# A graph network on one core: the attention stages' rows of edgeless nodes made in the gather windows instead of the first pass, with new orders in three other stages

## The reference

```python
h = relu(layernorm(x)); x = x + gcn2(h)          # two convolutions, 128 -> 256 -> 128, self loops
h = relu(layernorm(x)); x = x + sage2(h)         # two layers: mean of neighbours @ wl + b + h @ wr, relu
h = relu(layernorm(x)); x = x + edge3(h)         # three layers with edge features, each with a layernorm
h = relu(layernorm(x)); x = x + gat4(h)          # four attention layers, 2 heads, self loops
```

## Time and profile before

| | |
|---|---|
| median of three runs | 6671.95 us |
| the profiled execution: its own time, its span | 6683.69 us, 6681.9 us |
| busy: PE, PEld, DVE, ACT, POOL | 66%, 56%, 57%, 44%, 52% |
| granted clock of PE, mean | 0.848 |
| moved by DMA | 815.71 MB, 122 GB/s |

### The profile page before, as it was taken

One profiled execution on the slowest core, in us unless ns is written; L12 is line 12 of the kernel. 1 busy time (PEld: TensorE's weight loads), 2 busy tenths in 40 slices (PEclk: granted clock), 3 DMA queues, 4 the chain that ended last, 5 costly groups with the idle time before them and its releaser, 6 DMA issues. The chain is left out here.

```text
span 6681.9 us, 125449 instructions
## 1 busy us (share of the span) xinstructions
PE 4418.0 (66%) x28875; PEld 3717.4 (56%) x28950; DVE 3833.9 (57%) x13851; ACT 2944.6 (44%) x7261; POOL 3487.0 (52%) x4337
## 2 busy tenths in 40 slices
PE   4888888888788668877798966630660480282065
PEld 3666666666566666667787856630550370272065
DVE  5777777777544883347677767730650460261186
ACT  3777777777432333335576755530230130031043
POOL 3444444444470747327575665027457556556666
PEclk9999999999999659998999987765895795696576
DMA  3555555555442665448543444222232232232143
GB/s 98 184 187 187 187 187 186 186 186 186 128 115 70 198 181 136 115 122 218 151 118 96 113 113 116 82 69 53 73 95 53 61 103 58 51 102 70 43 115 91
DMA packets 1002707, 815.71 MB, mean 122 GB/s; under 512 B 103820, under 2 KB 836818, under 8 KB 1002616
## 3 DMA queue, kind: packets, MB, share of 16 engines
q1 hardware_dynamic: 908536, 650.27, 31.5%
q0 software_dynamic: 94080, 164.48, 10.3%
HBM read 359.28 MB, written 459.01 MB: 122 GB/s over the span
## 5 line engine op out<-in xcount | busy, mean ns | idle before, releaser
L839 POOL DMA_INDIRECT G<-table,idx_all x1568 | 1522.7, 971 | 1308.3 <-issue 670.6
L1411 PE MATMUL PS<-G,S 128*128 (+2 forms) x4312 | 852.3, 304 | 6.4 <-DMA G<-table,idx_all 2.4
L1411 PEld LDWEIGHTS PS<-G,S 128*128 128x128 f32 x4312 | 731.4, 220 | 55.8 <-issue 48.2
L839 POOL DMA_INDIRECT G<-table,idx_l x588 | 581.6, 989 | 336.2 <-issue 178.7
L1734 ACT ACTIVATE CR<-PS 65x128 f32<-65x128 f32 (+3 forms) x1078 | 289.1, 268 | 1021.2 <-PE PS L1411 1009.6
L1411 PE MATMUL PS<-CR,LO 97*128 97x128 f32 (+1 forms) x4312 | 655.3, 301 | 64.4 <-ACT CR L1734 64.4
L1408 PE MATMUL PS<-ident,ES 128*98 128x128 f32 x16 | 4.2, 420 | 1002.3 <-DVE ES L470 1002.3
L1411 PE MATMUL PS<-G,FS 128*65 (+2 forms) x3234 | 521.2, 301 | 216.9 <-DVE den L1343 100.7
L1411 PEld LDWEIGHTS PS<-CR,LO 97*128 97x128 f32 x4312 | 606.9, 217 | 75.7 <-ACT CR L1734 75.7
L792 POOL DMA_INDIRECT XIN<-in_x,idx_x x196 | 187.5, 957 | 846.0 <-ACT GN L1734 732.4
L470 DVE COPY ES<-G 128x392 f32<-128x392 f32 x4 | 2.1, 528 | 1016.5 <-DMA G<-table,idx_all 1016.5
(11 more groups left out here) (287 smaller groups left out, 11282.1 us busy)
## 6 DMA issues: line engine op xcount, KB each, us to landing
table<-G SPq DMA_DIRECT2D x392, 260.0 KB, 2.5
table<-G SPq DMA_DIRECT2D x392, 256.0 KB, 2.1
table<-RO SPq DMA_DIRECT2D x245, 256.0 KB
table<-RO SPq DMA_DIRECT2D x196, 260.0 KB
OWN<-table SPq DMA_DIRECT2D x196, 260.0 KB
XIN<-xrows SPq DMA_DIRECT2D x196, 256.0 KB
OWN<-table SPq DMA_DIRECT2D x147, 256.0 KB
xrows<-RB SPq DMA_DIRECT2D x147, 256.0 KB
```

Source lines behind the costliest of these rows:

```text
L839: g.indirect_dma_start(G[:, t, 0:w], None, TAB[s], bass.IndirectOffsetOnAxis(ap=idx[:, t:t + 1], axis=0)).then_inc(gat[t % 4].sem, 16)
L1411: return nc.tensor.matmul(o, l, r, start=start, stop=stop)
```

## The change

**Attention rows.** The plain stage now makes table 8 alone, and stores x in front of the fourth network (`x_plain`). Each attention stage s gets `beside_gathers(s)`, which all engines but POOL run ahead of `attention_middle`, while POOL gathers. In the three GA stages (kind "F") it goes over the 98 quads of plain nodes: SP loads rows of table s, PE turns them, ACT adds bias and relu, PE multiplies by the layer's weights, DVE copies 520 columns out of PSUM, SP stores them to table s + 1. There are four input buffers, two for the turned rows, two for output. In GZ (kind "FO") SP loads rows of table 11 and of `x_plain`, DVE adds the output bias and then both, SP stores the output; each of the three has four buffers.

**Plain stage.** Orders on all engines are new. The third norm is scaled by DVE (`normed`, four tensor_scalar of 128x128) in place of ACT, with the relu at PE's transposed rows; the sage bias comes by a bf16 matmul of 512 columns on PE (`ones_bias`, `eb2[:, 3]`) in place of an add on DVE; the attributes are copied by DVE in place of ACT. On POOL `cut_attributes` stands behind the node scatters and gathers.

**Edge stages.** The carries are taken out of the tile with j == 0 (`carries`, `next_carries`). C1 and S1 put all four tiles between the turn and the first products and the carries between the first and the second. LA and LB open their sum with the same bias matmul, and the add on DVE goes. LB's second norm is done one quad late for its statistics and two quads late for its scaled rows (`BEHIND = {"S2": 1, "LB": 2}`), with coefficients of its own (`sd2`, `rs2`, `nb2`) and two buffers (`LBU`), and S is made by one instruction instead of four.

**Before the loop** two more small loads and one more splitting of a weight into bf16 parts (of 512 columns) stand in the preparation.

```diff
+            def beside_gathers(s):              # SP
+                def load(m, k):
+                    if not isinstance(m, int) or m:
+                        used, step = (f_t, "turn") if kind == "F" else (f_v, "sum")
+                        sp.wait_ge(used.sem, used.at(ph, quad_of(m, k - 4), step))
+                    sp.dma_start(F_IN[kind][k], plain_rows(TAB[s], at(m, k) + EP)).then_inc(f_in[k].sem, 16)
...
+                def store(m, k):
...
+                    sp.wait_ge(f_v.sem, f_v.at(ph, quad_of(m, k), "rows" if kind == "F" else "sum"))
...
+                def step(m, k):
+                    here, behind = shifted(m, k, 0), shifted(m, k, 4)
+                    if here:
+                        load(*here)
+                    if behind:
+                        store(*behind)
...
+                def rows(m, k):
+                    dve.wait_ge(f_r.sem, f_r.at(ph, quad_of(m, k), "rows"))
+                    if not isinstance(m, int) or 4 * m + k > 1:
+                        q, b = shifted(m, k, 2)
+                        dve.wait_ge(f_st[b].sem, f_st[b].at(ph, q, "rows"))
+                    v.tensor_copy(F_OUT[k % 2][:, :, :], pair(2 + 2 * (k % 2))).then_inc(f_v.sem, 1)
...
                 if kind in ATTENDED:
+                    beside_gathers(s)
                     attention_middle(dve, v, link, s)
```

More of the change, by code:

```diff
@@ L134, in gnn_program @@
         eb1 = sb("eb1", [P, 3])
[L135 removed]
+        eb2 = sb("eb2", [P, 4, 4, D], bf16)
         lnw_c = sb("lnw_c", [P, 3])
@@ L416, in turn_of, with by_fours, shifted, quad_of @@
             return m + c if c else m
+        def by_fours(eng, body, ahead):
+            whole = PLAIN_QUADS // 4
+            for k in range(4):
+                body(0, k)
+            with eng.Fori(1, whole - 1) as m:
+                for k in range(4):
+                    body(m, k)
+            for i in range(4 * whole - 4, PLAIN_QUADS + ahead):
+                body(i // 4, i % 4)
+        def shifted(m, k, by):
+            i = k - by
+            if isinstance(m, int) and not 0 <= 4 * m + i < PLAIN_QUADS:
+                return None
+            return (m + i // 4 if i // 4 else m), i % 4
+        def quad_of(m, k):
+            return m * 4 + k
         loads = [(w1[:, :], a["L0_gnn_W1"]), (w2[:, :, :], a["L0_gnn_W2"].rearrange("(b p) c -> p b c", p=P)),
@@ L1462, in hidden @@
                 ready(pe, (q_a[1], q, "gT"))
-                before = earlier(q, 1)
-                if half and not q[2] and before is not None:
-                    alone(pe, (e_cp, turn_of(before) + 1))
                 mm(PS[:, 1 + half], w1[:, P * half:P * half + P], PT1[:, :]).then_inc(q_p[1].sem(q), 1)
@@ L1671, in tail_rows, with beside_gathers, turned, rows @@
                     rows4(pair(6, GW + 2), OT[:, :], WX[:, 0, :]).then_inc(pd.sem, 1)
+            def beside_gathers(s):
+                ph = ATTENTION.index(s)
+                if BESIDE[ph] != "F":
+                    return
+                def turned(m, k):
+                    pe.wait_ge(f_in[k].sem, f_in[k].at(ph, m, "rows"))
+                    for j in range(4):
+                        i = turn(PS[:, k % 2, P * j:P * j + P], F_IN["F"][k][:, j, 0:D])
+                    i.then_inc(f_t.sem, 1)
+                def rows(m, k):
+                    n = quad_of(m, k)
+                    pe.wait_ge(f_a.sem, f_a.at(ph, n, "hT"))
+                    if not isinstance(m, int) or 4 * m + k > 1:
+                        pe.wait_ge(f_v.sem, f_v.at(ph, n - 2, "rows"))
+                    rows4(pair(2 + 2 * (k % 2)), F_HT[k % 2], WX[:, ph + 1, 0:GW]).then_inc(f_r.sem, 1)
+                def step(m, k):
+                    here, behind = shifted(m, k, 0), shifted(m, k, 1)
+                    if here:
+                        turned(*here)
+                    if behind:
+                        rows(*behind)
+                by_fours(pe, step, 1)
             for s, kind in STAGES:
@@ L1722, in _ @@
                     tile(s, 0, 0, j)
+                carries(s, 0, 0)
                 quad(0, 0)
-                with pe.Fori(0, LAST // 2 - 1) as m:
+                quad(1, 1)
+                quad(2, 0)
+                with pe.Fori(1, LAST // 2 - 1) as m:
                     quad(m * 2 + 1, 1)
@@ L1938, in finish @@
                     ahead(2, 1)
-                    scaled(s, n, ACT.Identity, "", U)
+                    scaled(s, n, ACT.Identity, bank(2 * h))
                     ahead(0)
@@ L1983, in tail_out, with beside_gathers, turned @@
                     attention_rows(s, n, ad_t)
+            def beside_gathers(s):
+                ph = ATTENTION.index(s)
+                if BESIDE[ph] != "F":
+                    return
+                def turned(m, k):
+                    act.wait_ge(f_t.sem, f_t.at(ph, quad_of(m, k), "turn"))
+                    f(F_HT[k % 2][:, :], PS[:, k % 2, :], ACT.Relu, bias=gb_c[:, ph:ph + 1]).then_inc(f_a.sem, 1)
+                by_fours(act, turned, 0)
             for s, kind in STAGES:
@@ L2026, in _ @@
                 quad(0, 0)
-                with act.Fori(0, LAST // 2 - 1) as m:
+                quad(1, 1)
+                quad(2, 0)
+                with act.Fori(1, LAST // 2 - 1) as m:
                     quad(m * 2 + 1, 1)
```

556 lines of the change are left out of this document (364 added, 192 removed), and 1 row of the table ad.

## The result

The changed kernel takes 6337.6 us (median of four runs, 6324.8 to 6339.0), the kernel before 6670.3 on the same chip: ratio 0.950, 95% interval 0.948 to 0.951. It is faster, by 333 us where 397 were forecast, and inside the range. The profiled execution took 6337.75 us (span 6336.0) against the 6683.69 before: 346 us less.

| stage | before | after | change | forecast |
|---|---|---|---|---|
| all up to C1's first gather (preparation, plain) | 1756.4 | 1610.2 | -146 | -274 |
| C1 | 407.4 | 351.1 | -56 | -54 |
| C2, S2 together | 660.0 | 661.4 | +1 | 0 |
| S1 | 441.9 | 389.7 | -52 | -55 |
| LA, LA | 606.4 | 598.6 | -8 | +8 |

What follows compares the result with a forecast made beforehand. It took PE as nearly the bound in the plain stage, waits in C1 and S1, a chain through all engines in LB, and POOL's gathers alone opening attention stages. Terms summed to -397: 6672 - 397 = 6275 us; 8 in 10 within 6135 to 6445.

Steps and rivals of the forecast that it cites:

- One sign that the prediction had named for being wrong: Plain stage: the prediction called itself wrong if DVE was idle for more than a quarter.
- The loop through the second norm: Plain stage: closed loop over PE, ACT and DVE sets the body, 14.1 us with edge rows' statistics, 13.0 without.
- I add 0.4: Plain stage: allowance per body for PE work at half clock, giving 13.9 us a body.
- LB: Stage LB: one norm no longer waits for the other; quad 8.5 us with some half clock, 446 us, -127 us.
- Gather windows: GA stages: plain nodes' work nearly hidden beside POOL's gathers; window 258 us, +12 us each, +36 for three.
- the cap of the DMA engines at 0.80 of the time: Gather windows: 0.80 taken as the highest lasting DMA share, putting GA's transfers at 260 us and GZ's at 350.
- GZ: GZ's gather window: transfers lengthen it to 315 us, +69 us (+40 to +130); DVE's two adds hidden.
- The rival of the shared port: GZ's window: DVE's adds and GpSimd instructions exclude each other; window 381 us, kernel 6340 us; chance 3%.
- The windows as the bound: GA windows: late stores or half-clock PE make them 3.3 us a quad, +80 us three times, 6480 us; chance 17%.
- Slower by two output buffers: GA windows: landing of 6.8 us makes 4.0 us a quad; kernel slower only above that, 6700 us; chance 3%.
- The plain stage at DVE's own work: Plain stage: body falls to DVE's own work, 12.6 us or less, kernel 6140 us; chance 12%.
- keeps its waits: Plain stage: SP or POOL late by the cutting's new order, 15.5 us a body, kernel 6435 us; chance 7%.

Runs made afterwards that it cites:

- e3: Changed kernel with, in the plain stage, 16 identity turns on PE before the second norm's rows and SP's next load ahead of q3's store; ratio to kernel before 0.927.
- e1: Changed kernel with PE turning the identity 16 times while waiting for the second norm's rows in the plain stage; ratio to kernel before 0.948.
- e5: Changed kernel with PE's old order of work in C1 and S1; C1 405.1 us, S1 445.9 us, kernel 6452 us.
- e4: Changed kernel with PE turning the identity 16 times before the second norm's rows in LB; LB 437.2 us, ratio to kernel before 0.944.
- e11: Changed kernel with the plain stage's identity turns and earlier load, plus identity turns in LB; 6146.35 us, ratio to kernel before 0.921.
- e6: Changed kernel with POOL starting each attention stage's gathers only after all edgeless nodes' rows of that stage are stored; 7128 us.
- e10: Changed kernel with DVE adding only a quarter of each block beside GZ's gathers, all transfers kept; those gathers took 248 us.
- e12: Changed kernel with two input buffers instead of four beside the first three attention stages' gathers; GA stages took 538.2, 540.4 and 538.6 us.

## Why the prediction was right, and by which terms it was off

The forecast was 397 us and the change of the profiled execution 346. This is close in part by luck: the plain stage and LB fell short of their terms by 155 us together, and LA, GA and GZ beat theirs by 106. The terms of C1, S1 and the preparation were right by themselves. One sign that the prediction had named for being wrong came true: in the plain stage DVE is idle for 0.34 of the time, more than a quarter, and the first gather of C1 came at 1610 and not near 1482.

**The plain stage** (-280 forecast, with +6 for the preparation; -146 measured for both). The loop through the second norm was the right one: with the clock full and no late load its body is 13.8 us in e3, where my 13.0 and 14.1 make 13.6. The mis-sized term is the half clock, "I add 0.4". The two products behind the wait cost (981 - 632) x 4 = 1.4 us and (708 - 592) x 2 = 0.2 more than at full clock (632 ns is from the earlier trace rows, 592 the mean of the second one in e1 and e3), together 1.6. And a term was missing: SP's load stands behind the store of the third product, which waits for DVE's last step, so DVE got its rows 1.1 us a body too late (29.3 us in 26 bodies). Each delay hid part of the other, which is why undoing one brought 30 or 44 us and both 155. The preparation can be read from the first statistics of a plain quad on DVE, which start at 80.9 us where they started at 74.3: +6.7, as forecast.

**C1 and S1** (-54, -55): -56 and -52, and e5 gives both back. The forecast of the wait, 0.65 to about 0.3, was 0.21.

**LA** (+8 for both): -8. PE's busy time rose by 4.0 us in the first LA, less than the 0.22 us a quad (10.8) of the forecast, and its idle time fell by 6.9, from 22.6 to 15.7. The carries now come out of the tiles; whether this did it was not tried.

**LB** (-127): -100. The wait was the named one, DVE's messages for the edge product behind the turn of GN. Again the half clock was sized too small: e4 and e11 give 437, below the 446 forecast, so the clock costs 35 us of which I had 0.2 us a quad, 10 us. Without these 10 the forecast is 436.

**Gather windows** (+12 each): +3.7, +1.6 and +1.3 by the copy that ends them (249.7, 247.6 and 247.3 us after the first gather, 246.0 before). The term that was off is the cap of the DMA engines at 0.80 of the time: GA ran at 0.85, GZ at 0.94, e6 and e10 at 0.98 and 0.99. The output buffers were priced with a landing of 2.4 us. The stores of the first GA window took 3.5 (median), which by the same formula is 2.35 us a quad and 230 us for 98, in accord with the 228 between SP's first load and last store; DVE spent 147 us there waiting for its stores. Outside the window each GA stage became 4 to 6 us shorter. I have not traced this, and it is no more than the GA stages differ between the groups of runs.

**GZ** (+69): +23, of which the window has 20. By the same cap I had 315 us for the window, by transfers; it is 266, and not by transfers. These were priced too high as well: 280 us at full share, where 0.94 of 266.2 is 250. The rival of the shared port was right in that VectorE's adds lengthen the indirect DMAs, with a wrong price; that a port is what they share was not tested. The Trainium skill (SBUF — State Buffer, Who interferes with whom) says that an add with two inputs in SBUF contends only with those GpSimd instructions that read SBUF, and expects no stall of descriptor writing by it. The prediction had left this condition out. In the runs indirect DMAs, which take their offsets from SBUF, became 85 ns longer in the mean beside 136 us of adds. That fits the first statement if it is the reading of the offsets that waits; no run tells which step of the instruction became longer. A whole blocking, priced at 135 us, is not seen either: in the changed kernel 145 of the 195 gathers of this window stayed below 1.1 us and the longest was 1.43.

**The rivals.** The windows as the bound: refuted by e6 (208 of 246 us) and e12. Slower by two output buffers: they do set the pace of the work, but at 2.35 us a quad and not at 4.0, which stays inside the gathers' time. The plain stage at DVE's own work (12.6 us or less a body): not reached, neither in the changed kernel nor in e3 (13.8). The plain stage "keeps its waits" at 15.5 us came closest to the measured body, 15.38: SP was late, as it said, though with the load of x and not by the cutting, and it did not name the clock: undoing the late load alone brought 44 of the 155 us.

## What to carry to other kernels

When work is taken from PE, its clock can fall in the waits that open, as it did here in the plain stage (0.89) and in LB (0.85): price the products behind such a wait at both levels, above all where they are on the chain that sets the next wait. Sixteen turns into an unused bank in that wait were worth 111 us here once the second delay was gone, and 30 before; two delays in one loop are to be tried together before either theory is dropped. Queue a load ahead of a store that waits for the end of the body. A window that only waits for gathers took 98 quads of load, product and store almost free of charge.

## What the runs showed that I had not expected

- The DMA engines can be busy for 0.98 to 0.99 of some 200 to 250 us (367 to 372 GB/s), and POOL's indirect DMAs issued beside it are not slowed by that: 947 ns each at a share of 0.99, 944 at 0.22.
- VectorE's adds of two SBUF blocks of 512 columns lengthen POOL's indirect DMAs: 944, 1029 to 1069, 1100 ns with 0, 136, 194 us of them. Its copies out of PSUM don't: in the GA window, with 68.6 us of them, the 196 gathers took 185.2 us, 945 ns each. The adds of 128 columns (57.4 us) hardly do: 947 ns, the longest 1044.
- The half level followed PE's waits wherever they moved: behind 2.97 us for ACT in the changed kernel w1's product took 3.20 us, behind 2.27 us for DVE in e1 the 16-part product took 3.61, and in e3 the clock was 1.00 with 62.0 us of idle time left in 400 (40.0, 15.4 and 6.6), no wait of it longer than 1.4 us.
